# Layer 0's stack of rows copied into PSUM by ScalarE, the transposes moved to layer 1's accumulator, and zero rows in the half tiles' fine weights

## The reference

```python
x0 = xk = e
for idx, (W, b) in enumerate(params):
    z = relu(einsum('bhd,bkd,hks->bsd', x0, xk, W) + b[None, :, None])
    if idx != 2:
        xk = z[:, :64, :]
        direct.append(z[:, 64:, :])
    else:
        direct.append(z)
logit = sum(concatenate(direct, axis=1), axis=-1)
```

## Time and profile before

| | us |
|---|---|
| median of 3 runs | 1316.96 (1316.22 to 1317.09) |
| the profiled execution | 1315.29 |
| its span | 1313.4 |
| PE busy | 1218.1 (93%) |
| DVE busy | 1144.2 (87%) |
| POOL busy | 1071.1 (82%) |
| ACT busy | 568.2 (43%) |
| granted TensorE clock | 0.996 of 2.4 GHz, mean |

### The profile page before, as it was taken

How to read it: one execution, slowest core, us unless ns; L and a number is a source line. 1 busy time by engine, 2 the same in 40 slices (tenths; PEclk the granted TensorE clock), 3 DMA queues, 4 the chain that set the end, 5 groups by cost and what they waited for, 6 DMA issues and landing times.

```text
span 1313.4 us, 15206 instructions
## 1 busy us (share of the span) xinstructions
PE 1218.1 (93%) x3912; PEld 723.5 (55%) x3912; DVE 1144.2 (87%) x911; ACT 568.2 (43%) x576; POOL 1071.1 (82%) x639
## 2 busy tenths in 40 slices
PE   0378999999999999999999999999999999999899
PEld 0144655656565565656565565656566565656555
DVE  1369998999999999999999899999999999999762
ACT  1044444454444444454444445444444445445443
POOL 6789899888989898898989988898989886656571
PEclk9989999999999999999999999999999999999999
DMA  4771807345280816437190724628081643715000
GB/s 118 251 268 40 321 6 256 108 159 204 52 312 7 291 67 213 151 106 257 36 326 4 257 106 153 210 55 308 7 301 58 209 154 91 269 61 183 0 1 1
DMA packets 81244, 196.26 MB, mean 149 GB/s; under 512 B 23984, under 2 KB 35343, under 8 KB 81194
## 3 DMA queue, kind: packets, MB, share of 16 engines
q1 hardware_dynamic: 70953, 193.14, 42.7%
q0 software_dynamic: 10240, 2.64, 2.1%
HBM read 193.17 MB, written 12.78 MB: 157 GB/s over the span
## 4 chain that ended last, share of the span: by engine, by line
PE 56%; DVE 14%; issue 13%; POOL 13%; ACT 3%; DMA 1%; DVEq 0%; SPq 0%; POOLq 0%; ACTq 0%
PE acc L840 53%; DVE prod L727 8%; POOL emb L454 7%; POOL lo L464 5%; DVE lo L740 3%; ACT hi L596 2%; DVE xk L727 2%; DVE hi L737 1%; DMA x_rows<-x_rows 0%; DMA x_tiles<-x_rows 0%; POOL pairs_r L484 0%; PE acc L894 0%; PE xk L894 0%; PE acc L921 0%; DVEq L724 0%
## 5 line engine op out<-in xcount | busy, mean ns | idle before, releaser
L464 POOL TENSOR_TENSOR lo<-prod,hi 128x1024 fp32r<-128x1024 f32 (+1 forms) x288 | 705.3, 2452 | 144.2 <-ACT hi L596 140.7
L727 DVE TENSOR_TENSOR prod<-x_tiles,xk 128x1024 f32<-128x1024 f32 x531 | 627.5, 1215 | 77.7 <-PE acc L840 53.3
L840 PE MATMUL acc<-prod,wfull 128*128 128x512 f32 (+2 forms) x1408 | 661.8, 594 | 0.0
L596 ACT ACTIVATE hi<-prod 128x1024 fp32r<-128x1024 f32 (+1 forms) x291 | 307.9, 1059 | 476.1 <-DVE prod L727 392.5
L454 POOL DMA_INDIRECT emb<-table,block_idx x320 | 334.7, 1046 | 66.9 <-issue 57.4
L840 PEld LDWEIGHTS acc<-prod,wfull 128*128 128x128 f32 (+2 forms) x1408 | 265.9, 190 | 205.3 <-issue 178.4
L840 PE MATMUL acc<-hi,whi 128*128 128x512 f32 (+1 forms) x800 | 350.7, 445 | 25.1 <-ACT hi L596 25.1
L840 PE MATMUL acc<-lo,whi 128*128 128x512 f32 (+1 forms) x736 | 303.6, 500 | 30.2 <-POOL lo L464 28.6
L840 PE MATMUL acc<-hi,wlo 128*128 128x512 f32 (+2 forms) x800 | 314.4, 399 | 0.0
L840 PEld LDWEIGHTS acc<-lo,whi 128*128 128x128 f32 (+1 forms) x736 | 135.1, 189 | 174.0 <-POOL lo L464 81.3
L727 DVE TENSOR_TENSOR prod<-x_stack,x_tiles 117x1024 f32<-117x1024 f32 (+1 forms) x112 | 200.7, 1857 | 28.4 <-DMA x_tiles<-x_rows 28.3
(11 more groups left out here) (70 smaller groups left out, 236.0 us busy)
## 6 DMA issues: line engine op xcount, KB each, us to landing
x_tiles<-x_rows SPq DMA_DIRECT2D x304, 512.0 KB, 9.7
x_rows<-x_rows SPq DMA_DIRECT2D x16, 624.0 KB
x_tiles<-x_rows SPq DMA_DIRECT2D x32, 256.0 KB, 11.4
x_stack<-x_rows SPq DMA_DIRECT2D x48, 156.0 KB
emb<-table,block_idx POOLq DMA_INDIRECT x320
x_rows<-x0T SPq DMA_DIRECT2D x64, 32.0 KB
x_tiles<-w SPq DMA_DIRECT2D x1, 768.0 KB, 5.8
x_tiles<-w SPq DMA_DIRECT2D x1, 704.0 KB, 8.4
```

The source lines that it names most:

```text
L464: nc.gpsimd.tensor_tensor(lo[0:r, product_slot(j), :], prod[0:r, product_slot(j), :], hi[0:r, part_slot(j), :].bitcast(f32), ALU.subtract) ...
L596: nc.scalar.activation(hi[0:r, part_slot(j), :], held(n, parity, j)[0:r, :], ACT.Copy).then_inc(hi_ready, 1)
L727: nc.vector.tensor_tensor(held(n, parity, j)[0:r, :], in0, in1, ALU.mult).then_inc(product_ready, 1)
L840: mm = nc.tensor.matmul(z[:, c], w[0:r], part[0:r, c], start=first and i == 0, stop=last and i == len(weights) - 1)
```

## The change

ACT copies `x0_stack` into xk[0] at the end of layer 1, once layer 1's products have been made, and layer 0's products read that copy. As xk[0] is no longer free in layer 0, the transposes go to accumulator(2, parity), which is layer 1's accumulator, after L0+4 and once z1 is evacuated; ACT's `copy_rows` moves to after the rounding of L2+0, and PE waits for it before it begins layer 2. `sum_direct2` moves on DVE from the middle of layer 1 to just ahead of L0+0. The wlo of the half tiles gets zeros in its lower 64 rows, and PE multiplies it by all 128 rows, together with whi, when the lower half is ready. The number of matmuls stays.

```diff
-SPLITS = [[t for t, k in enumerate(ks) if k != "F"] for ks in KINDS]
+SPLITS = [[t for t, k in enumerate(ks) if k in "GD"] + [t for t, k in enumerate(ks) if k == "H"] for ks in KINDS]
...
+            def copy_stack(n):
+                act.wait_ge(stack_loaded, PER * 16 * (n + 2))
+                if not is_step(n, PROLOGUE):
+                    act.wait_ge(product_ready, reached(n, L0 - 1, "FDGH"))
+                nc.scalar.activation(xk[0][0:ROWS0, :], x0_stack[0:ROWS0, :], ACT.Copy).then_inc(stack_copied, 1)
...
             copy_rows(0, xk[0], reuse=False)
+            act.wait_ge(rows_copied, 1)
+            copy_stack(PROLOGUE)
...
-                round_hi(n, parity, L1 + Z2_AFTER, L0 + XK1_AFTER)
+                round_hi(n, parity, L1 + Z2_AFTER, L0)
+                copy_stack(n)
+                round_hi(n, parity, L0, L0 + XK1_AFTER)
                 evacuate(1, n, z1, reached(n, L0 - 1, "FDGH"), copied=2)
                 round_hi(n, parity, L0 + XK1_AFTER, L0 + DIRECT1_AFTER)
                 evacuate_direct1(z1)
-                round_hi(n, parity, L0 + DIRECT1_AFTER, L0 + COPY_AFTER)
+                round_hi(n, parity, L0 + DIRECT1_AFTER, L2 + COPY_AFTER)
                 if not past_end(n, 2):
-                    copy_rows(n + 2, xk[0])
+                    copy_rows(n + 2, z1)
...
-                in0, in1 = (x0_stack[0:r, :], tile) if l == 0 else (tile, xk[l - 1][0:r, :])
+                in0, in1 = tile, xk[max(l - 1, 0)][0:r, :]
...
                     if l == 0:
                         if t == 0:
-                            dve.wait_ge(stack_loaded, PER * 16 * (n + 2))
+                            if not is_step(n, PROLOGUE):
+                                sum_direct2(n)
+                            dve.wait_ge(stack_copied, n + 2)
...
-                    if l == 1 and t == T1 // 2:
+                    if l == 1 and t == T1 // 2 and past_end(n, 1):
                         sum_direct2(n)
...
-                    multiply(j, [whi[:, w, :]], part, False, False).then_inc(tile_used, tiles)
+                    multiply(j, [whi[:, w, :]] + [wlo[:, w, :]] * (KIND[j] == "H"), part, False, False).then_inc(tile_used, tiles)
...
-                        pe.wait_ge(hi_ready, reached(n, j, "DGH"))
-                        if KIND[j] == "H":
-                            multiply(j, [wlo[:, w, :]], hi[:, part_slot(j), :], False, False, r=NEXT)
-                        else:
+                        if KIND[j] != "H":
+                            pe.wait_ge(hi_ready, reached(n, j, "DGH"))
                             multiply(j, [whi[:, w, :], wlo[:, w, :]], hi[:, part_slot(j), :], j == start, False)
...
                     contract(n, L0, L2, accumulator(0, parity), None if past_end(n, 2) else
-                             (L0 + 1, lambda: transpose_rows(n + 2, parity, xk[0])))
+                             (TRANSPOSES_AFTER, lambda: transpose_rows(n + 2, parity, accumulator(2, parity), n + 1)))
                 pe.wait_ge(z_evacuated[1], n + 1)
+                if not past_end(n, 2):
+                    pe.wait_ge(rows_copied, n + 3)
```

More of the change, by code:

```diff
@@ L241, in build @@
         stack_loaded = sem("stack_loaded")
+        stack_copied = sem("stack_copied")
         tile_loaded = [sem(f"tile_loaded{q}") for q in range(SLOTS)]
@@ L650, in _ @@
             copy_rows(1, xk[1])
-            XK1_AFTER, DIRECT1_AFTER, COPY_AFTER = 3, 4, 5
+            XK1_AFTER, DIRECT1_AFTER, COPY_AFTER = 3, 4, 2
             Z0_AFTER, Z2_AFTER = 5, 4
@@ L678, in step @@
                 evacuate_direct1(z1)
-                round_hi(n, parity, L0 + DIRECT1_AFTER, L0 + COPY_AFTER)
+                round_hi(n, parity, L0 + DIRECT1_AFTER, L2 + COPY_AFTER)
                 if not past_end(n, 2):
-                    copy_rows(n + 2, xk[0])
-                round_hi(n, parity, L0 + COPY_AFTER, L2 + Z0_AFTER)
-                evacuate(0, n + 1, z0, reached(n, L2 - 1, "FDGH"), copied=None if past_end(n, 2) else n + 3)
+                    copy_rows(n + 2, z1)
+                round_hi(n, parity, L2 + COPY_AFTER, L2 + Z0_AFTER)
+                evacuate(0, n + 1, z0, reached(n, L2 - 1, "FDGH"))
                 round_hi(n, parity, L2 + Z0_AFTER, STEP)
@@ L713, in _ @@
                 dve.wait_ge(whi_ready, l + 1)
-                part = slice(SPLIT_AT[l], SPLIT_AT[l] + len(SPLITS[l]))
+                part = slice(SPLIT_AT[l], SPLIT_AT[l] + len(SPLITS[l]) - (l > 0))
                 r = rows(l, 0)
+                if l:
+                    half = SPLIT_AT[l] + SPLITS[l].index(SHORT)
+                    nc.vector.tensor_tensor(wlo[0:NEXT, half, :], w_stage[0:NEXT, half, :],
+                                            whi[0:NEXT, half, :].bitcast(f32), ALU.subtract)
+                    nc.vector.memset(wlo[NEXT:128, half, :].bitcast(f32), 0.0)
                 nc.vector.tensor_tensor(wlo[0:r, part, :], w_stage[0:r, part, :], whi[0:r, part, :].bitcast(f32),
@@ L819, in _, with transpose_rows @@
         def _(pe):
-            def transpose_rows(m, parity, target):
+            TRANSPOSES_AFTER = L0 + 4
+            def transpose_rows(m, parity, target, evacuated=None):
+                if evacuated is not None:
+                    pe.wait_ge(z_evacuated[1], evacuated)
                 pe.wait_ge(rows_gathered[parity], 8 * PAIRS * (m + 2 - parity))
@@ L834, in contract, with multiply @@
                 columns = [slice(c * BANK, (c + 1) * BANK) for c in range(COLS // BANK)]
-                def multiply(j, weights, part, first, last, r=None):
-                    r = r or rows(*ORDER[j])
+                def multiply(j, weights, part, first, last):
+                    r = rows(*ORDER[j])
                     for c in columns:
```

## The result

| | before | after |
|---|---|---|
| median, us (4 runs each) | 1316.59 (1315.78 to 1317.09) | 1279.66 (1279.44 to 1280.98) |
| ratio | | 0.9722 [0.9707, 0.9737] |
| the profiled execution, us | 1315.29 | 1279.59 |
| its span, us | 1313.4 | 1277.7 |

The change saves 2.8%: 35.7 us between the two profiled executions, 36.9 between the medians. The forecast was 1281.0.

The account below looks back on a forecast made before the run. PE was taken as nearly full, losing time in layer 0 to late POOL lo; 24.8 + 1.6 + 6.6 + 0.8 + 2.5 = 36.3 us off the 1316.96 median gave 1281 us, forecast range 1274 to 1288, 8-in-10 range 1272 to 1299.

Parts of the forecast that it names:

- The products' term: Layer 0: products reading PSUM remove PE's waits for POOL's lo, 24.8 us in steps 0 to 12, 1.6 in 13 and 14.
- floor of 11.71 for layer 0: Layer 0's length in us without its net loss of 1.91 us, from PE's load distances; it lasted 13.62.
- worst case of 0.12 to 0.3: Layer 0: smallest predicted margins in us, 0.12 at L0+0, 0.3 for the waits on POOL's two lo.
- ACT's copy: End of layer 1: copying the stack takes 1.07 us beside DVE's subtraction and sum, so costs nothing.
- price of 1.1: In front of L0+0: us the stack's copy would cost without DVE's subtraction and sum as cover.
- Rival A: First product of layer 0: cover fails, a new wait of some 1 us in 15 steps, 1296 us; chance 0.14.
- The transposes: After L0+4: same three instructions, ACT's copies done 2.5 us before PE wants layer 2, so no cost.
- rival B: Start of layer 2: PE waits for ACT's copies, 3.0 us in 14 steps, slower at 1323 us; chance 0.07.
- Zero rows: H tiles: 0.41 us each goes, 6.6 in layer 2, 0.8 in layer 1 of steps 14 and 15 only.
- Rival C: H tile: its full-height loads are exposed, so 6.6 and 0.8 nearly vanish, 1288 us; chance 0.05.
- Start: Prologue: POOL's three gathers behind the products get faster, worth 2.5 us, between 0 and 2.8.
- Rival D: Layer 1 loosens too, POOL reaching L1+15's lo in time: 0.59 + 0.41 more in 14 steps, 1267 us; chance 0.07.

Follow-up runs that it names:

- Run 3: Changed kernel with DVE's layer-0 products reading the stack in SBUF again, ACT's copy, moved sum and moved transposes kept: 1314.55 us.
- run 4: Kernel before with the zero rows and the direct2 sum moved in front of L0+0, stack in SBUF, transposes after L0+1: 1308.94 us.
- Run 10: Changed kernel with the sum of direct2 back in the middle of layer 1: 1279.14 us.
- Run 9: Changed kernel with the transposes after L0+6 instead of L0+4, directly before layer 2: 1294.84 us.
- run 1: Kernel before with only the zero rows added: 1310.02 us, ratio 0.9951.
- run 5: Changed kernel with one gather of a step moved from layer 1 to layer 2: 1267.13 us.
- run 7: Changed kernel with two gathers of a step moved from layer 1 to layer 2 and the H tiles as before the change: 1278.54 us.
- run 8: Changed kernel with the H tiles' wlo matmuls on 64 rows inside the lo part, so instructions alternate 128, 64, 128, 64 rows: 1293.78 us.

## Why the prediction was right

The sum was 36.3 between profiled executions, and 35.7 came out. By the starts of the layers it consists of 26.5 in layer 0, 6.9 in layers 2 and 1 (the H tiles) and 2.3 before layer 0 of step 0; the errors of the terms are small, and partly offset one another.

**The products' term** was 24.8 + 1.6. Measured by the layer's length: 1.92 in each of 13 steps, 0.77 and 0.82 in steps 13 and 14, 26.5 together. Run 3 shows that the operand in SBUF is what makes the wait, and runs 4 and 10 that the moved sum is not. The prediction's floor of 11.71 for layer 0 is met to the hundredth, since it was made of PE's own rows. The margins were better than the worst case of 0.12 to 0.3 that the prediction worked out: 1.49 us at L0+0, and 1.68 and 1.06 at the two `lo` (549.85 for 551.53, 555.30 for 556.36). Of the sum's two microseconds one came free earlier: DVE's last subtraction begins 6.79 us before PE's layer 0 (542.10 for 548.89), where it was 5.72 (559.21 for 564.93).

**ACT's copy** was taken as 1.07 and took 1.03, at no cost. Run 10 takes the sum's 1.95 out of the cover and loses nothing, since the subtraction, 1.22, is enough. The price of 1.1 with no cover at all was not tested; it was reckoned against a margin of 0.12, and the margin was 1.49. Rival A's condition did not arise.

**The transposes** were costed at nothing, with 2.5 us to spare. In the trace ACT ends the second copy at 558.41 and PE loads for layer 2 at 560.60: 2.2. Run 9 takes the cover away and shows that the time would have been 1.1 a step: by that price rival B could not have made the kernel slower than before, since 14 x 1.1 = 15 is less than the gain. The step of it that failed is the assumption that product and rounding of L2+0 would stand in the round trip; they are done long before (the 5.24 of run 9). What the prediction did not see is that the transposes had been filler in the wait that the change removes (run 3); it made no difference as the wait went too.

**Zero rows.** 6.6 + 0.8, and 5.8 and 7.1 measured, 6.9 in the trace of the change, since an H tile costs 0.38 to 0.39 and not 0.41. That layer 1 would swallow its half was the least certain step, and runs 1, 5 and 7 settle it: 0.38 a step while POOL's chain binds, 0.78 once it doesn't, and PE's wait at the lo of L1+15 grew from 0.91 to 1.33, by the amount of the zero rows. Rival C fell with the nine distances of 0.23 at the H tile, and run 8 shows what costs instead. 128-row loads behind 128-row matmuls are hidden, 0.23 apart, and a change between 128 and 64 rows is not, whichever way. This is against what the Trainium skill says of loads that overlap only where row groups differ ("TensorE: Matmul & The Clock Gate", Part 3, The mechanism); the same section also lets a load into the background weight buffer go ahead, and the hidden loads do not speak against that. The trace agrees with the Trainium skill's sentence "Changing tiling mode (not just tile) drains the TensorE" ("TensorEngine Tiling (Array Packing)", Key Properties), with 0.2 us for one such change here, if a matmul of 64 rows counts as another mode; that it does is not shown.

**Start.** 2.5 was taken. Layer 0 of step 0 starts 2.28 earlier. POOL's three gathers take about 0.95 each, where they took 1.77 to 1.96 (the earlier trace rows have one):

```profile
56.28 0.96 POOL L455 DMA_INDIRECT emb<-table,block_idx  x1
...
58.80 0.95 POOL L455 DMA_INDIRECT emb<-table,block_idx  x1 [0.30 <-issue]
...
76.54 2.37 POOL L465 TENSOR_TENSOR lo<-prod,hi 128x1024 fp32r<-128x1024 f32 x1
```

The first lo of layer 1 starts at 76.54, and at 78.84 in the trace before. The traces of different runs scatter here by 1 us and more (115.17 and 116.10 in runs 1 and 4), but most of that lies ahead of PE's first layer 0. Counted from there, layer 0 of step 0 comes after 61.11 to 61.49 us in the four traces with the stack in SBUF, run 3's among them, and after 58.28 to 58.44 in the eight with it in PSUM. So the term is about 2.7, close to the 2.8 reckoned from the three gathers, and 0.44 of it is lost here because PE's first layer 0 starts later (53.78 for 53.34).

**Rival D** was half right: layer 1 does not loosen by itself, but run 5 loosens it by moving one gather, for the 0.98 a step that the rival named (0.59 + 0.41).

## What to carry to other kernels

Where VectorE and GpSimd work side by side, as here, try one operand of VectorE's two-tensor instructions in PSUM: the copy on an idle ScalarE cost nothing, and both engines got back more busy time than the kernel gained. Build the floor of a stage from the tensor engine's load distances, and subtract what a late group makes good; the difference tells what a removed wait is worth. Ask for each stage anew whose chain ends last there: the same 0.4 us was worth all of it in layer 2 and nothing in layer 1, until one gather was moved.

## What the runs showed of the hardware that was not expected

A change between 128 and 64 rows from one matmul to the next costs about 0.2 us in either direction, also when it goes from the smaller to the larger (run 8: load distances of 0.43 for 0.23), so four instructions that alternate cost twice what two in a row do. Not every change of the number of rows does this. In the changed kernel's layer 0 the 128-row transposes stand among 117-row matmuls (557.03, 0.24 after the load before), the 78-row ones follow 117-row ones (558.88, 0.43 after), and 128 rows follow 78 (560.60, 0.43 after): all at the usual distance. Between 78 and 64 rows no run looks. The transposes, 128 and 64 columns wide, show no such gap either (0.45 to 0.46 for three).
